# Two self-attentions whose loop over groups of heads is a machine loop, and the same loop written out

## The reference

```python
x = _layernorm(x + _L0_attn_ref(x, L0_attn_Wq, ...), axis=-1)
...
# layer 1, differential attention: 2 x 16 score heads of 8, 16 value heads of 16
def attend(qh, kh):
    scores = jnp.einsum('bthd,bshd->bhts', qh, kh) * SCALE
    p = jax.nn.softmax(scores, axis=-1)
    return jnp.einsum('bhts,bshe->bthe', p, v12)
a = attn1 - lam * attn2
```

## Time and profile before

| what | us |
|---|---|
| median of three timed runs | 4248.61 |
| the three runs | 4248.61, 4248.86, 4227.96 |
| profiled execution, its own time | 4232.43 |
| its span in the trace | 4230.7 |
| TensorE, VectorE, ScalarE, GpSimd busy | 3516.9, 2917.2, 1941.1, 766.1 |
| mean granted TensorE clock | 0.894 of full |

### The profile page before, as it was taken

The page is one execution under the profiler, slowest core; times in us unless marked ns, Lnnn a source line. Parts: engine busy times, 40 slices in busy tenths (PEclk is TensorE's granted clock), DMA queues, the critical chain, the costliest instruction groups (busy, mean ns, idle before and its releaser), DMA issues. The chain is left out here.

```text
span 4230.7 us, 63916 instructions
## 1 busy us (share of the span) xinstructions
PE 3516.9 (83%) x19000; PEld 1700.2 (40%) x19000; DVE 2917.2 (69%) x4353; ACT 1941.1 (46%) x3763; POOL 766.1 (18%) x1063
## 2 busy tenths in 40 slices
PE   7599999766478885999999999999965769999758
PEld 4244444433234352333333333333333435554625
DVE  6557676346546687988888888888745457776374
ACT  2156666222111032777777777777741213334121
POOL 3222223123300051000000000000022434445000
PEclk9669999788789996999999999999987879999678
DMA  5311121000010061000000000000000231110202
GB/s 196 112 36 47 46 46 31 18 35 10 0 41 15 20 198 38 23 19 17 20 22 17 21 21 17 23 19 17 10 3 29 88 123 42 28 36 1 88 17 71
DMA packets 81131, 175.80 MB, mean 42 GB/s; under 512 B 21592, under 2 KB 39008, under 8 KB 79424
## 3 DMA queue, kind: packets, MB, share of 16 engines
q1 hardware_dynamic: 79968, 165.76, 12.9%
q10 hardware_dynamic: 864, 6.29, 0.4%
HBM read 87.76 MB, written 54.72 MB: 34 GB/s over the span
## 5 line engine op out<-in xcount | busy, mean ns | idle before, releaser
L631 DVE TENSOR_REDUCE L_attn_tops<-L_attn_psM 128x2 f32<-128x1024 f32 (+3 forms) x1408 | 1560.9, 1148 | 337.3 <-PE L_attn_psM L741 329.2
L568 ACT ACTIVATE L_attn_E<-L_attn_psS 128x512 f32<-128x512 f32 (+3 forms) x2816 | 1389.3, 575 | 583.4 <-PE L_attn_psS L700 580.0
L700 PE MATMUL L_attn_psS<-L_attn_Q,L_attn_K 64*128 64x512 f32 (+3 forms) x2816 | 995.5, 437 | 108.0 <-ACT L_attn_E L568 40.1
L741 PE MATMUL L_attn_psM<-L_attn_K,L_attn_Q 62*128 62x512 f32 (+3 forms) x2816 | 1023.6, 484 | 57.1 <-DMA L_attn_K<-parts_k 30.0
L700 PEld LDWEIGHTS L_attn_psS<-L_attn_Q,L_attn_K 64*128 64x128 f32 x2816 | 474.4, 192 | 806.1 <-ACT L_attn_E L568 634.1
L716 PE MATMUL L_attn_psO<-L_attn_E,L_attn_V 128*32 128x512 f32 (+3 forms) x5632 | 738.6, 598 | 0.0
L741 PEld LDWEIGHTS L_attn_psM<-L_attn_K,L_attn_Q 62*128 62x128 f32 x2816 | 433.9, 195 | 170.4 <-DVE L_attn_tops L631 53.0
L526 POOL TENSOR_TENSOR L_AO<-L_attn_o 128x128 f32 (+1 forms) x64 | 29.4, 459 | 1463.2 <-DVE L_attn_o L664 1463.2
L1436 PE MATMUL m_psE<-m_we,m_xT 128*128 128x512 f32 x512 | 235.1, 619 | 0.0
L535 POOL TENSOR_SCALAR_AFFINE_SELECT L_attn_E<-L_attn_E 128x128 f32<-128x128 f32 x512 | 146.6, 293 | 458.6 <-ACT L_attn_E L568 447.4
L2134 ACT ACTIVATE x_E<-x_psS 128x512 f32<-128x512 f32 x256 | 138.9, 595 | 175.3 <-PE x_psS L2257 158.0
(11 more groups left out here) (339 smaller groups left out, 3787.7 us busy)
## 6 DMA issues: line engine op xcount, KB each, us to landing
parts_q<-L_proj_parts SPq DMA_DIRECT2D x64, 256.0 KB
parts_k<-L_proj_parts SPq DMA_DIRECT2D x64, 256.0 KB
L_attn_Q<-parts_q SPq DMA_DIRECT2D x192, 64.0 KB
L_attn_K<-parts_k SPq DMA_DIRECT2D x192, 64.0 KB
L_attn_Q<-parts_q SPq DMA_DIRECT2D x64, 128.0 KB
L_attn_K<-parts_k SPq DMA_DIRECT2D x64, 128.0 KB
queries<-x1p_qo SPq DMA_DIRECT2D x16, 512.0 KB
keys<-x1p_ko SPq DMA_DIRECT2D x16, 512.0 KB
```

Of the source, the lines that this page charges most:

```text
L568: act.activation(E[(4 * n + s) % 8][:, c0:], psS[bank][:, c0:], ACT.Exp, scale=scale).then_inc(e_done, 1)
L631: dve.tensor_reduce(dst, src, AX, ALU.max).then_inc(m_read, 1)
L700: pe.matmul(psS[bank][:, c0:], K[g.slot][r:r + RH, c, kt * P:(kt + 1) * P], Q[g.slot][r:r + RH, c, q * HALF + c0:(q + 1) * HALF], start=Tr ...
L741: last = pe.matmul(psM[bank][:, j * HALF:j * HALF + n], Q[t.slot][r:r + TOP, c, qt * P:(qt + 1) * P], K[t.slot][r:r + TOP, c, h * HALF:h * ...
```

## The change

`run` no longer calls `run_turns`. It is a plain loop in the generating program, so that all turns (18 in layer 0, 34 in layer 1) stand one after another in each engine's stream, with constants for every address and count. The conditions on `t.n` and `g.n` go, since n is always None. `run_turns` itself stays for the other sublayers. The diff at its core (the same edit of the call to `run` is in all five engines' parts):

```diff
-        def run(eng, turn):
-
-            run_turns(eng, lambda t, live: turn(t, *live), groups, 2, 3)
+        def run(turn):
+
+            for g in range(groups + 2):
+                turn(At(g, None, 3), g < groups, 1 <= g <= groups, g >= 2)
...
-            if t.n is None and t.base < 2:
+            if t.base < 2:
                 return j, j % 3
...
-            if t.n is None and t.base == groups + 1:
+            if t.base == groups + 1:
...
-                    if g.base >= 3 or g.n is not None:
+                    if g.base >= 3:
                         sp.wait_ge(s_done, s_item(g + -1, 4 * LATE + 1)[0])
...
-                    if g.base >= 1 or g.n is not None:
+                    if g.base >= 1:
...
-                        if t.n is not None or t.base >= 1 or p >= 2:
+                        if t.base >= 1 or p >= 2:
                             pe.wait_ge(m_read, i + -1)
...
-                run(sp, turn)
+                run(turn)
```

More of the change, by code:

```diff
@@ L548, in turn @@
                         combine_heads(t, t + -1, 0, at["back0"])
-                run(pool, turn)
+                run(turn)
                 if shared == 2:
@@ L592, in turn @@
                             evacuate(t + -1, 0)
-                run(act, turn)
+                run(turn)
             @block.vector
@@ L683, in turn @@
                         combine(t, at)
-                run(dve, turn)
+                run(turn)
             @block.tensor
@@ L779, in turn @@
                             turn_back(t, t + -1, 0, at["back0"])
-                run(pe, turn)
+                run(turn)
 LAMBDA_INIT = 0.8 - 0.6 * math.exp(-0.3 * 12)
```

## The result

| | median us | lowest, highest | runs |
|---|---|---|---|
| before | 4233.9 | 4228.0, 4248.9 | 9 |
| changed | 4214.6 | 4194.1, 4240.4 | 9 |

What follows compares the result with a forecast made beforehand. It took TensorE's stalls at layer 1's loop jumps, with clock dips behind them, as the removable cost. 42.5 us less 2.5 that stay gave 40.0, other terms 0: 4192.4 or 4208.6, middle 4200 us, range 4178 to 4226.

Steps and rivals of the forecast that it cites:

- rival A: Layer 1: the clock dips stay and only the stall goes; gain 26 us, 4206 or 4223 us; chance 0.10.
- (1): Layer 1's loop: its nine jumps go on all engines, with the stall and the dip behind it; 42.5 us in total.
- (2): Layer 1: two late landings of the rows of maxima, beside instruction fetches, stay; 2.5 us of the 42.5.
- (3): Looped turns: register instructions ahead of the waits cost 0.01 us a turn, 0.3 us over 27; nothing added.
- (4): Layer 0's three jumps: gain of 0 to 1.5 us cancels against about 1 us of late-landing waits; taken as 0.
- (5): Fetching straight code: layer 1's loop is refetched anyhow, so writing it out costs 0.
- B: Layer 0's kind of clock dip comes into layer 1: 13 dips, 52 us, so 12 us slower; chance 0.07.
- C: Late landings of the maxima spread to 34 more turns, 41 us, leaving no gain: 4233 or 4249 us; chance 0.05.
- D: Layer 1: idle on issue is not the jump's and stays; gain 0 to 1.3 us, 4231 to 4249; chance 0.05.

## Why the prediction was right, and where it was not

The time fell in the range and the sign was right, and the stall was the right cause. That the number came so close is in part luck. The forecast of 4200 stood half way between two levels, 4232.4 and 4248.6; the median of nine runs of before is 4233.9, and 40.0 us off that is 4194, so the forecast gain was 20.7 us too large and not 14. The 4214.6 lies outside the forecast's own range of 4182 to 4212. It is in the full range only since that was drawn wide enough for rival A, and A is not what happened. Behind it stand two errors, one of them mine in reading code.

**How far the loop reaches, in the account of the kernel and in the first part: wrong.** `run_turns(eng, turn, groups, 2, 3)` passes lag 2 and step 3; `first` is left at 0. I took `first` for 3. So only turns 0 and 1 are written out before the loop in layer 1 and turns 0 to 3 in layer 0, not 0 to 4 and 0 to 6. The loop makes ten iterations (turns 2 to 31) and four (4 to 15). What I called three written-out turns, 1692.45 to 1823.64, was the loop's first iteration. The figures stand as measured, but the argument built on them, "the kernel already holds both versions of the code", was empty: it compared the loop with itself. The 42.5 us came out right all the same, as that first iteration follows no jump back and the nine others do. The stall after 1823.64 was not at a jump into the loop but at the first jump back; nine jumps is right for ten iterations. In the account of the change, the listings headed "turn 5" show the start of turn 2, and what they call turn 4 is turn 1. The trace could have said so, since the register instructions stand in ScalarE's stream already in turn 3. In the same way the 102.30 us of layer 0's "written-out" turns 4 to 6 were an iteration.

**(1), the jumps: right.** 42.5 us was the price of nine jumps: TensorE's stalls with their dips, and some 9 us that ScalarE's own jumps still cost once TensorE's were gone. Swapping two waits brought layer 1 to 44.0 us less, and five jumps less brought 21.7.

**(2), two late landings that stay:** the changed kernel has three waits for `mparts` on L701, 1.1 us in all, for two and 2.4. Too small to settle.

**(3), register arithmetic at zero: this is the step that failed.** It was costed by setting looped turns against looped turns. The register instructions themselves are cheap: with the waits swapped, a turn without them takes 43.64 us, 0.09 less than looped. But the one ahead of the exponential did a service: it carried the early wait. With it gone, both waits met on the exponential and the late one was split off. The term is +0.79 us a turn, 23.6 us over 30 turns. The order printed ahead of the prediction even showed the row with `o_done` and `s_done` on one exponential, above the words "Between two activations nothing is left". On TensorE and VectorE few waits were split (seven and four instructions of this kind in a turn of layer 1, against ScalarE's sixteen), and the run with TensorE alone shows no such price there.

**(4), layer 0 at zero: right in the median** (0.9992), though not for the reason given, a small gain that late landings cancel. A turn there at full clock takes 32.34 us, against 32.56 before, so the straight code gains there two tenths of a microsecond a turn. The clock dips outweigh that. The changed kernel (windows of two turns and of one dip):

```profile
298.61:330.95 32.34, 31.23 (x235) 14.08 (x235) 23.97 (x33) 21.42 (x52) 9.72 (x33) 1.00 0.23 51
330.95:369.98 39.03, 36.78 (x235) 16.16 (x235) 24.22 (x33) 22.00 (x52) 9.67 (x33) 0.83 0.19 42
554.20:578.00 23.80, 23.80 (x113) 10.32 (x114) 11.67 (x14) 11.38 (x25) 5.17 (x17) 0.50 0.24 53
```

and a looped turn of before:

```profile
454.49:487.05 32.56, 31.26 (x237) 14.14 (x235) 23.94 (x33) 21.49 (x52) 9.74 (x33) 1.00 0.23 50
```

A turn with a dip takes 39.03 us for 32.34. There were six dips in this execution, one of them 23.9 us long, and four of 10.2 us before. What times them I did not settle. They differ between kernels whose layer 0 is the same code (before and layer 1 alone: 529.7 and 519.6 us from the first to the last `negm`), so they are a likely part of the spread of all these runs.

**(5), fetching straight code at zero: right.** TensorE alone written out runs turns of 43.73 us.

**Rivals.** A fell: the dips went with the stalls, in 1420 us of layer 1 there is none. B fell by the same window, 1201.83 us at 1.00. C fell: TensorE waited three times for `mparts`, 1.1 us in all, where C needed 34 waits. D fell: the idle on issue is gone, and the branch instruction itself took the time. What happened was none of the four. Its 23.6 us are more than the 14 that A would have kept.

## What to carry to other kernels

When a loop is written out, look at what carried the waits: two waits that used to stand on a register instruction and on the work now share one instruction, and the one that comes late should be placed so that it rides on the work itself (here: the first `wait_ge` ahead of it in the source). What a jump costs goes with the length of the body on its engine, and each engine has its own measure: here TensorE stood 3.0 us at a body of 1909 recorded instructions and 0.2 us at one of 1667, while ScalarE lost 2.4 us and more even at 338, of which 0.5 to 1.0 us a jump came through to the turn. So the price is to be read at the jump, engine by engine. And before a stretch of a trace is taken as the reference for "without the loop", the loop's bounds should be read off the trace itself.

## What the runs showed of the hardware

- A second wait on an instruction can cost time. Split off as its own instruction it makes the exponential start 0.06 us later where it is the late one (0.77 us a turn over sixteen, 0.05 each), and nothing measurable where it is the early one: 44.41 against 43.64 us a turn for the same waits in another order. The Trainium skill, "Perfetto Trace Analysis", section Identifying Dependency Chains, says that such instructions may be inserted; which wait goes where, and the price, are from these runs.
- TensorE's jump back over three turns of layer 1 costs 3.0 us idle on issue, over six turns of layer 0 2.7 us, over three turns of layer 0 about 0.2 us on its weight loads. Its branch instruction is recorded with 3.5 to 4.0, 3.6 and 0.22 us.
- At ScalarE's jump back the next recorded instruction comes 2.5 to 2.8 us after the branch in layer 1 (446 recorded instructions from jump to jump, the run with TensorE alone) and 2.4 to 2.6 us in layer 0 (338, before). On VectorE, GpSimd and SyncE (140 to 299 in layer 0, 29 to 256 in layer 1) it comes within 0.3 us. With bodies of six turns VectorE is late too, by 2.8 to 3.0 us (382 and 509), and GpSimd in layer 0, by 3.4 us (596). SyncE at 278 was late once, by 2.5 us in layer 0, and not in layer 1, so the recorded length alone doesn't decide there.
- The half-clock (1.2 GHz) dips of layer 1 follow the stalls: nine before, none over 1420 us once TensorE doesn't stall. A stall need not bring one: with layer 0 alone and with ScalarE alone written out there are eight dips behind nine stalls, and the turns with the stall and no dip took 47.20 and 47.08 us, where those with both took 47.5 to 49.5. In layer 0, dips of 6.8 to 23.9 us come without any jump.
